# K projection of the next tile evacuated ahead of the norm of the current tile, in an FFT-attention and expert layer on 8 cores

## What is computed

```python
def attn(x, Wk, bk, Wv, bv, Wq, bq):
    k = jnp.fft.fft(x @ Wk.T + bk)
    v = jnp.fft.fft(x @ Wv.T + bv)
    q = jnp.fft.fft(x @ Wq.T + bq)
    kv = jnp.cumsum(k * v, axis=1)
    queried = kv * jnp.conj(q)
    nrm = jnp.sqrt(jnp.sum(jnp.abs(queried) ** 2, axis=-1, keepdims=True))
    return jnp.real(jnp.fft.ifft(queried / (1e-09 + nrm))) / np.sqrt(x.shape[-1])
x = x + attn(layernorm(x), ...)      # x is (4, 8192, 1024) f32
x = x + ffn(layernorm(x), ...)       # shared expert and 8 routed experts, hidden 2048
```

## Time and profile before

| what | us |
|---|---|
| median of 2 runs | 4844.97 (4837.35 to 4852.59) |
| the profiled execution | 4840.11 |
| its slowest core's span (core 7) | 4839.1 |
| spans of the other cores | 4803.5 to 4830.6 |
| TensorE busy on core 7 | 3907.5 (81%) |
| VectorE, ScalarE, GpSimd busy | 1091.5, 522.7, 190.7 |

### The profile page before, as it was taken

The page is one execution under the profiler, slowest core; times in us unless marked ns, Lnnn a source line. Parts: engine busy times, 40 slices in busy tenths (PEclk is TensorE's granted clock), DMA queues, the critical chain, the costliest instruction groups (busy, mean ns, idle before and its releaser), DMA issues.

```text
span 4839.1 us, 46593 instructions; the slowest of 8 cores (4803.5 to 4839.1 us)
## 1 busy us (share of the span) xinstructions
PE 3907.5 (81%) x17976; PEld 1716.4 (35%) x17976; DVE 1091.5 (23%) x2177; ACT 522.7 (11%) x817; POOL 190.7 (4%) x362
## 2 busy tenths in 40 slices
PE   4468531358888299999969999988999996999998
PEld 1123210123333144444434444433444443444444
DVE  0141210123333321122231122222112223111111
ACT  1110110123333110000010100001010001110000
POOL 0000000000000010000000100001000000110000
PEclk8779765678888599999989999999999998999999
DMA  5430799951111221322122222221232212213111
GB/s 87 91 100 1 91 118 117 117 96 44 44 44 36 96 94 41 107 111 83 44 105 79 78 97 100 101 74 59 72 113 79 89 73 83 92 53 113 70 72 68
DMA packets 62681, 391.16 MB, mean 81 GB/s; under 512 B 9712, under 2 KB 9712, under 8 KB 50688
## 3 DMA queue, kind: packets, MB, share of 16 engines
q0 software_dynamic: 34720, 287.45, 24.4%
q1 hardware_dynamic: 26752, 100.67, 6.2%
q10 hardware_dynamic: 992, 0.07, 0.0%
HBM read 423.81 MB, written 88.08 MB: 106 GB/s over the span
## 4 chain that ended last, share of the span: by engine, by line
PE 71%; DMA 7%; DVE 6%; another core or an unknown queue 6%; ACT 3%; issue 3%; DVEq 2%; ACTq 1%; POOL 0%; SPq 0%; POOLq 0%
PE ps_r L1086 18%; PE ps_tb L1086 18%; PE ps_a L1010 4%; PE ps_tb L1010 4%; PE ps_r L1016 4%; PE ps_id L355 4%; PE ps_b L1016 3%; PE ps_r L1053 2%; PE ps_tb L1053 2%; PE ps_id L512 2%; PE ps_q L355 2%; DMA w<-w2s 2%; DMA wab<-wabs 1%; PE ps_tr L556 1%
## 5 line engine op out<-in xcount | busy, mean ns | idle before, releaser
L1086 PE MATMUL ps_r<-w,hsT 128*128 128x512 bf16 x4096 | 915.2, 382 | 24.8 <-DMA w<-w2s 24.8
L1086 PE MATMUL ps_tb<-w,hsT 128*128 128x512 bf16 x4096 | 904.9, 379 | 0.0
L1086 PEld LDWEIGHTS ps_r<-w,hsT 128*128 128x128 bf16 x4096 | 403.0, 98 | 516.8 <-issue 40.3
L1086 PEld LDWEIGHTS ps_tb<-w,hsT 128*128 128x128 bf16 x4096 | 400.8, 98 | 483.3
L355 PE MATMUL ps_kv<-wtk_b,xT_b 128*128 128x512 bf16 x512 | 132.1, 417 | 317.0 <-ACT xT_b L352 317.0
L1094 DVE SCALAR_TENSOR_TENSOR acc<-ps_tb,wse,acc 128x1024 f32<-128x1024 f32 x128 | 164.3, 1284 | 719.7 <-PE ps_tb L1086 719.7
L1094 DVE SCALAR_TENSOR_TENSOR acc<-ps_r,wse,acc 128x1024 f32<-128x1024 f32 x128 | 164.3, 1284 | 662.0 <-PE ps_r L1086 662.0
L1010 PE MATMUL ps_a<-hiT,wab 128*128 128x512 bf16 x1024 | 244.0, 394 | 41.4 <-ACT glog L917 19.8
L355 PE MATMUL ps_id<-wtv_b,xT_b 128*128 128x512 bf16 x512 | 182.8, 536 | 99.6 <-ACT kvs_b L390 99.6
L1010 PE MATMUL ps_tb<-hiT,wab 128*128 128x512 bf16 x1024 | 233.0, 381 | 16.3 <-DMA wab<-wabs 14.4
L1016 PE MATMUL ps_r<-hiT,wab 128*128 128x512 bf16 x1024 | 231.5, 379 | 0.0
(11 more groups left out here) (204 smaller groups left out, 2686.6 us busy)
## 6 DMA issues: line engine op xcount, KB each, us to landing
w<-w2s POOLq DMA_DIRECT2D x72, 2048.0 KB, 12.0
wab<-wabs POOLq DMA_DIRECT2D x256, 256.0 KB, 3.0
w2s<-w2T POOLq DMA_DIRECT2D x8, 4096.0 KB, 377.0
xf<-xp SPq DMA_DIRECT2D x32, 512.0 KB, 3.4
xf<-x SPq DMA_DIRECT2D x32, 512.0 KB, 4.2
x1s<-x_sb SPq DMA_DIRECT2D x32, 512.0 KB, 5.0
acc<-x1s SPq DMA_DIRECT2D x4, 4096.0 KB, 15.4
x1t<-x1s SPq DMA_DIRECT2D x32, 512.0 KB, 10.9
```

Of the source, the lines that this page charges most:

```text
L1086: mi = PE.matmul(pr[:, 512 * h:512 * (h + 1)], hsT[:, hc * CH + i * 128: hc * CH + (i + 1) * 128], w2_b[bi][:, hc * D + 512 * h: hc * D + ...
```

## The change

`p_projK(t+1)` and `a_evacK(t+1)` are called ahead of `a_norm(t)` and `d_qn(t)`, and no longer behind them. No instruction is added or taken away, and no wait. TensorE has no call between the old and the new place, so its order stays as it was. On ScalarE one copy (L390) goes from behind the norm's instructions to ahead of them.

```diff
@@ -713,11 +713,12 @@
                 if t + 1 < NT:
                     a_evacX(t + 1)
                 a_evacCQ(t)
+                if t + 1 < NT:
+                    p_projK(t + 1)
+                    a_evacK(t + 1)
                 a_norm(t)
                 d_qn(t)
                 if t + 1 < NT:
-                    p_projK(t + 1)
-                    a_evacK(t + 1)
                     p_projV(t + 1)
                     a_evacV(t + 1)
                 p_trQ(t)
```

## The result

| what | before | changed |
|---|---|---|
| undisturbed executions, us | 4836 to 4853 | 4732 to 4745 |
| the profiled execution, us | 4840.1 | 4729.3 |
| ratio, 95% interval | | 0.9785 (0.9764 to 0.9805) |
| the same, second set of runs | | 0.9778 (0.9754 to 0.9801) |
| slowest core's span, us | 4839.1 (core 7) | 4728.2 (core 2) |

The median over all 11 runs of the changed kernel is 5062.5 us and that of 10 runs of before is 4913.4 us: in about half of the executions of either kernel the cores of one die (four of the eight cores) or of both ran at a lower clock, and the ratio is made from the others, here called undisturbed. By the ratio the kernel became 2.15% faster, 104 us of 4840, where 108 us were worked out; between the two profiled executions it is 110.8 us. The interval reaches from 1.95% to 2.36%.

The account below looks back on a forecast made before the run. TensorE was taken to bound the attention loop behind the weight copying, with a gap before V and a lowered clock. 48.9 + 58.8 + 0.3 = 108.0 us off 4840.1 gave 4732 us; range 4718 to 4770.

Parts of the forecast that it names:

- The bound: In the attention loop behind the weight copying, TensorE sets the time, idle 3.47 us before V and slowed after it.
- the second stretch: Core 7's attention loop from 1032.8 to 1596.1 us: DMA share 0.14, TensorE busy 473 of 563 us, clock 0.85.
- The gap of 1.41 us: TensorE's idle before the V projection falls from 3.47 to 1.41 us in 23 passes: 48.9 us less.
- The clock: V projection on TensorE runs at full clock after the shorter gap, busy as long as Q: 58.8 us less.
- The six rows: Six gaps of 1.41 to 1.42 us before V, on four cores in the first stretch; all kept the clock.
- What is now late: ScalarE's norm starts 0.90 us later, behind the copy of K; V hides it with 1.10 us to spare: 0 us.
- The first stretch: Attention loop from 527 to 1009 us, DMA share 1.00, tiles waiting for x: 0 us from seven passes in the wait.
- the edge: At the edge of the seven passes hidden by the wait for x, one pass may give 0.3 us.
- The falling clock: TensorE's clock still falls after the shorter gaps before V: 4771 us in every pass, 4752 in half; chance 0.27.
- The other three: Gain taken back at loop's end or by loads, 4791 us (0.06); late transpose, 4868 us (0.02); another wait before V (0.03).

## Why the prediction was right, and where it was wrong

*The bound.* Right. The gap before V and the slow V behind it were the loss of the second stretch, and the kernel that only fills the gap shows that they are cause and effect.

*The gap of 1.41 us.* Right: 48.9 us were worked out and 48.7 measured. The two handovers and the copy are the same wherever ScalarE is free.

*The clock.* Right in its size (58.8 and 58.9 us), and in its doubt. Of 182 V projections on eight cores one was slow. Four gaps were longer than 1.42 us (1.50 to 1.57), and it followed one of them, on core 7:

```profile
1318.35 5.30 PE L355 MATMUL ps_id<-wtv_b,xT_b 128*128 128x512 bf16 x16 [1.51 <-ACT kvs_b L390]
```

So taking the row nearest in length and in make-up held, but by little, and in part by luck: 0.04 us more of gap would have turned the answer. The six rows were also less alike than the prediction says. In all of them K ran at half clock for most of its length, and the clock rose only 1.1 to 1.3 us before K's end, while in the second stretch TensorE is at full clock all along. Core 1 of before, the K projection ahead of the V at 612.16, columns as in the earlier trace rows:

```profile
603.79:609.50 5.71, 5.71 (x14) 2.02 (x15) 3.37 (x9) 2.35 (x3) 0.00 (x0) 0.50 1.13 136
609.50:610.75 1.25, 1.25 (x5) 0.21 (x3) 0.00 (x0) 0.99 (x4) 0.00 (x0) 0.99 0.73 88
```

That both kinds of gap were answered alike was a guess that came true. The Trainium skill, page "TensorE: Matmul & The Clock Gate", section "A second HAM failure mode: psum-queue depth-cycling", has the clock swing with repeated small idles. The runs agree at 1.46, 1.48 and 1.90 us with the bias last, and show no such swing at 1.41 us, nor at 1.48 us with dense matmuls up to the gap.

*What is now late.* Right. From K's end the transpose came at + 5.50 us (+ 5.49 worked out). Scaling ended at + 3.94 us; with the handover of 0.35 that leaves 1.21 us to spare (1.10 worked out), because the norm starts 0.91 us after the copy and not 1.01.

*The first stretch.* Right: 80 to 81 us a pass as before, the gain there only lengthened the wait for x (from 59.5 to 62.3 us in the pass that was read). For single cores the edge was sized too small: I gave it 0.3 us, and the loop's end moved by 95.0 to 120.9 us from core to core, since the last slow load lets a core go at another moment. In the mean over the cores it is 107.4 us, so the edge cancels out.

*The forecast and its range.* The mechanism, the pass (19.16 us) and the sum held: 4732.1 us for an execution like the profiled one, 4729.3 us measured. That these two lie only 3 us apart is partly luck. The slowest core is another one after the change (2, not 7). Between the two, the second stretch gave 107.1 us, its start came 2.8 us later, and the FFN, which the prediction put at nothing, was 6.5 us shorter. The step that failed is the one from the profiled execution to the kernel's time. I set the two equal to within 5 us, and made the sum from 4840.1, because two executions of before lay 15 us apart. But over more executions the median is 4913 us before and 5062 us for the changed kernel, 292 us above the range's upper end: 73 us of the difference to the forecast were missing in the starting value already, and the rest comes from where the median falls among the executions of the changed kernel. Two values say nothing of how the middle of many falls. For the ratio, in which a change is judged, the step did no harm.

*The rivals.* The falling clock is the one that was near: it costs 1.7 us in 16 or 17 of 23 passes at 1.46 us, 29 us where I had put 19 to 39. The other three did not occur.

## What to carry to other kernels

When one engine's queue holds an operation that waits for a third party ahead of a copy that the matmul engine waits for, put the copy first, and price the gap twice: once as idle time, once as the clock behind it. A gap that repeats in each pass is worth closing by any useful work, and what can't be moved away from it should be dense matmuls, with one-row ones elsewhere. Before relying on a gap that is just short enough, lengthen it by a few hundredths of a microsecond and look.

## What the runs showed of the hardware that I had not expected

- The clock's answer to a gap is sharp in time: gaps of 1.41 to 1.42 us kept it in every pass of the changed kernel's second stretch (178 in its first profile, 175 in the second), 1.46 us lost it in 16 or 17 of 23 on each of eight cores. It is not monotone: at 1.90 us 11 or 12 were lost, at 3.47 us nearly all. Why 1.90 us is milder than 1.46 us was not settled; at 1.90 us the slow passes alternate with full ones.
- Two one-row matmuls ahead of the gap count against it. At 1.90 us their place changes 11 or 12 slow V projections of 23 into 0 to 2.
- A drain on ScalarE cost 0.04 us, and a copy of one column ahead of a copy of 1024 columns only 0.06 us, where the rows of one-column operations show 0.16 to 0.20 us.
